# Attention in a macaron transformer: where VectorE frees a PSUM bank, and in which steps it adds gathered expert rows

## The reference, cut to what matters

```python
# mixture of experts: x = x + 0.5 * sum over the two best experts of weight * expert(norm(x))
# attention, on norm(x):
q = (x @ Wq + bq).reshape(b, t, H, hd).transpose(0, 2, 1, 3)
k = ((x @ Wk + bk) @ Wl + bl).reshape(b, t, H, lhd).transpose(0, 2, 1, 3)
v = ((x @ Wv + bv) @ Wl + bl).reshape(b, t, H, lhd).transpose(0, 2, 1, 3)
attn = jax.nn.softmax(jnp.einsum('bhqd,bhkd->bhqk', q, k) * scale, axis=-1)
out = jnp.einsum('bhqk,bhkd->bhqd', attn, v)
x = x + out.transpose(0, 2, 1, 3).reshape(b, t, L) @ Wo + bo
```

## Time and profile before

| | |
|---|---|
| median of 3 runs | 1384.77 us (1379.14 to 1384.81) |
| profiled execution, its own time | 1381.53 us |
| its span, first to last instruction | 1379.8 us |
| mean granted TensorE clock | 0.962 |
| busy over the span | PE 89%, DVE 81%, ACT 63%, POOL 37% |
| the chain that ended last, by engine | PE 54%, DVE 25%, issue 8%, ACT 8% |

### The profile page before, as it was taken

How to read it: one execution, slowest core, us unless ns; L and a number is a source line. 1 busy time by engine, 2 the same in 40 slices (tenths; PEclk the granted TensorE clock), 3 DMA queues, 4 the chain that set the end, 5 groups by cost and what they waited for, 6 DMA issues and landing times.

```text
span 1379.8 us, 22519 instructions
## 1 busy us (share of the span) xinstructions
PE 1227.8 (89%) x7168; PEld 776.2 (56%) x7168; DVE 1120.5 (81%) x2387; ACT 875.9 (63%) x1535; POOL 511.8 (37%) x762
## 2 busy tenths in 40 slices
PE   6767989678899879988889999899999899899998
PEld 5657989412322322222267999866666356656675
DVE  6865979789989979888767989978886787778885
ACT  6855777358788858887887777634343588234432
POOL 6772437544544506420373335605330220210100
PEclk9988999779999989999999999999999999999999
DMA  8595556522312203210263566456463010263535
GB/s 271 122 362 188 210 196 231 157 73 89 93 48 90 82 26 97 86 48 14 74 229 120 198 220 216 138 125 136 96 136 67 10 43 19 44 128 78 117 71 122
DMA packets 116608, 167.94 MB, mean 122 GB/s; under 512 B 18884, under 2 KB 63460, under 8 KB 115468
## 3 DMA queue, kind: packets, MB, share of 16 engines
q1 hardware_dynamic: 109324, 151.82, 37.7%
q0 software_dynamic: 7168, 14.69, 3.6%
HBM read 80.72 MB, written 45.09 MB: 91 GB/s over the span
## 4 chain that ended last, share of the span: by engine, by line
PE 54%; DVE 25%; issue 8%; ACT 8%; POOL 3%; DMA 2%; SPq 0%; DVEq 0%; ACTq 0%; POOLq 0%
PE bank L1703 8%; DVE shared L2326 6%; PE bank L2404 5%; PE pair L1615 4%; PE pair L1617 4%; PE pair L1616 3%; PE pair L955 3%; PE pair L957 3%; PE pair L2386 3%; PE pair L956 3%; PE pair L2318 3%; DVE shared L1039 3%; ACT shared L2394 2%; POOL xs_rows L649 2%; DVE shared L1037 2%
## 5 line engine op out<-in xcount | busy, mean ns | idle before, releaser
L2326 DVE TENSOR_REDUCE shared<-pair 128x2 f32<-128x1024 f32 x256 | 309.9, 1217 | 37.9 <-PE pair L2318 34.8
L2394 ACT ACTIVATE shared<-pair 128x1024 f32<-128x1024 f32 x256 | 260.6, 1021 | 49.8 <-PE pair L2386 48.0
L955 PE MATMUL pair<-shared 128*128 128x256 f32 (+1 forms) x704 | 225.5, 320 | 6.8 <-issue 3.6
L957 PE MATMUL pair<-shared 128*128 128x256 f32 (+1 forms) x704 | 215.9, 307 | 0.0
L956 PE MATMUL pair<-shared 128*128 128x256 f32 (+1 forms) x704 | 215.6, 306 | 0.0
L1039 DVE TENSOR_TENSOR shared<-shared 128x512 fp32r<-128x512 f32 x208 | 155.9, 757 | 56.3 <-ACT shared L1029 53.1
L1670 ACT ACTIVATE shared<-pair 128x512 f32<-128x512 f32 x144 | 84.6, 594 | 146.9 <-PE pair L1617 144.8
L1615 PE MATMUL pair<-shared 128*128 128x512 f32 x288 | 152.4, 529 | 0.2 <-DVE shared L1625 0.2
L1023 ACT ACTIVATE shared<-pair,shared 128x256 f32<-128x256 f32 x288 | 121.5, 477 | 48.9 <-PE pair L957 42.5
L955 PEld LDWEIGHTS pair<-shared 128*128 128x128 f32 x704 | 136.0, 193 | 15.0 <-issue 5.4
L2404 PE MATMUL bank<-shared 128*9 128x512 f32 x1024 | 137.1, 608 | 4.5 <-ACT shared L2394 4.3
(11 more groups left out here) (384 smaller groups left out, 2249.6 us busy)
## 6 DMA issues: line engine op xcount, KB each, us to landing
shared<-shared SPq DMA_DIRECT2D x144, 256.0 KB
shared<-p_coef_rows SPq DMA_DIRECT2D x64, 512.0 KB, 8.6
shared<-xs_rows SPq DMA_DIRECT2D x36, 256.0 KB, 3.0
ys_rows<-shared SPq DMA_DIRECT2D x36, 256.0 KB
w_keep<-shared SPq DMA_DIRECT2D x8, 1024.0 KB, 13.8
shared<-w_keep SPq DMA_DIRECT2D x16, 512.0 KB
shared<-p_q_parts SPq DMA_DIRECT2D x64, 96.0 KB, 2.3
shared<-p_k_parts SPq DMA_DIRECT2D x64, 96.0 KB, 2.4
```

Source lines behind the costliest of these rows:

```text
L955: nc.tensor.matmul(out_bank, w_hi, x_hi, start=start, stop=False)
L957: return nc.tensor.matmul(out_bank, w_lo, x_hi, start=False, stop=stop)
L2326: nc.vector.tensor_reduce(mneg[:, i, 2 * c:2 * c + 2], pair_of("max", b, m)[:], AX_X, ALU.max, negate=True).then_inc(s["mx_read"], 1)
L2394: nc.scalar.activation(probs[st % 2][:, 2 * p:2 * p + 2, :], pair_of("exp", b, 2 * st + p)[:], ACT.Exp, scale=scale).then_inc(s["exp_done" ...
```

## The change

VectorE's turn operations move in front of the maximum of the same slot, and the eight adds of a body move from slots 13 to 23 to slots 1 to 9. No operation is added or removed on any engine, and no size changes.

```diff
@@ -2561,17 +2561,22 @@
                         if st == 15:
                             norm_from(f0 + b + AHEAD, b + AHEAD, bank[7])
 
+            def turn_dve(v, b, at, first_):
+                st, j = divmod(at, 2)
+                if j == 0 and st % TILES == 3:
+                    if st > 3:
+                        o_dve(v, b, st // TILES - 1)
+                    elif not first_:
+                        o_dve(v, b - 1, GB - 1)
+                if at == 10 and not first_:
+                    z_dve(v, b - 1)
+                if at == 18 and b + FIRST < B:
+                    v_dve(v, b + FIRST, bank[7])
+
             def between_dve(v, b, st, j, first_):
                 g, kt = st // TILES, st % TILES
                 at = 2 * st + j
                 routed = routes is not None and not first_
-                if j == 0 and kt == 3:
-                    if st > 3:
-                        o_dve(v, b, g - 1)
-                    elif not first_:
-                        o_dve(v, b - 1, GB - 1)
-                if at == 10 and not first_:
-                    z_dve(v, b - 1)
                 if routed and b in PLACED_IN and at in PLACED_IN[b][1]:
                     G, pieces = PLACED_IN[b]
                     place, half = pieces[at]
@@ -2581,8 +2586,6 @@
                     seq_stats_a(v, routes, b - 1)
                 if routed and at == 12:
                     seq_stats_b(v, routes, b - 1)
-                if b + FIRST < B and at == 18:
-                    v_dve(v, b + FIRST, bank[7])
                 if b + AHEAD < B:
                     if at in COMBINE_AT:
                         combine_piece(v, occ0, b + AHEAD, COMBINE_AT.index(at))
@@ -2597,11 +2600,12 @@
                     if routes and b == B - 1 and st == 15:
                         weights_dense(v, routes)
 
-            COMBINE_AT = (13, 15, 16, 17, 19, 20, 21, 23)
+            COMBINE_AT = (1, 2, 3, 4, 5, 7, 8, 9)
 
             def dve_b(v, b, par, first_, last_):
                 for st in range(STEPS):
                     for j in range(2):
+                        turn_dve(v, b, 2 * st + j, first_)
                         if lagged(b, 2 * st + j):
                             max_dve(v, *lagged(b, 2 * st + j))
                         between_dve(v, b, st, j, first_)
```

## The result

The changed kernel takes 1373.45 us (median of 11 runs, 1369.73 to 1377.39), the kernel before 1381.27 in its own 11 (1378.97 to 1384.81): a ratio of 0.9946, 95% interval 0.993 to 0.9962. It is faster, by 7.5 us by that ratio (the medians are 7.8 apart), where 18.2 were forecast. Its profiled execution took 1375.78 us, span 1374.0.

The account below looks back on a forecast made before the run. TensorE and VectorE were both taken as within 10% of full, VectorE saturated in slots 11 to 25. Gains of 14.5 us in the bodies and 3.7 for the clock, 18.2 together, took 1384.77 to 1366.6 us; range 1359 to 1379.

Parts of the forecast that it names:

- What bounds the kernel: Attention bodies: TensorE and VectorE within 10% of full; VectorE has spare time in slots 0 to 9, none in 11 to 25.
- Part 1, which waits go: Turns before maxima: 23.2 of 25.6 us of TensorE's bank 7 waits can go; new VectorE waits priced at nothing.
- Part 1, what is given back: Bodies 1 and 2: late maxima delay score matmuls, 1.1 of 3.8 us lost, 2.7 gained each, about 47.0 us long.
- Body 6: Waits of 1.1 us go, less 0.5 at slot 30, where the score matmul waits for the delayed maximum: 0.6 gained.
- Body 3: Gains 2.7 us like bodies 1 and 2, and 1.2 at its end: 3.9.
- Part 2, the adds: Eight adds in bodies 0 to 4 move to early slots, costing nothing in bodies 0 to 3; body 4 gains 1.0 us from both parts.
- rival (d): Gathers block adds: three a body, up to 0.98 us each, 13 us over five bodies, half in idle time: 1373; chance 0.03.
- Part 3, the clock: End of body 3: gap shrinks from 2.57 to 1.35 us, so TensorE's clock no longer falls to half; 3.7 us gained.
- (a): The clock falls all the same at the end of body 3: 1370.3 us; chance 0.15.
- (b): Early slots have no room, VectorE becomes the bound there, adds cost 10.5 us of the gain: 1377; chance 0.10.
- (c): The order gives nothing, TensorE waits for later maxima instead of the bank; only collisions go: 1381; chance 0.13.
- (e): Adds and placement in slots 3 to 9 stretch TensorE gaps in bodies 0 to 4, the clock falls: 1393; chance 0.05.

Follow-up runs that it names:

- e2_adds: Only the adds moved, turn operations still behind the maximum, against the kernel before; 1378.31 us, ratio 0.9962.
- e3_pool: The changed kernel, with POOL splitting the maxima of group 3 before the gather of slot 15; 1369.37 us, ratio 0.9905 to the kernel before.
- e8_slot30: The changed kernel, with `o_dve` behind the maximum again in slot 30 of body 6 alone; 1372.82 us, ratio 0.9933 to the kernel before.
- e10_before: The kernel before, unchanged, measured and traced a second time; 1382.43 us, ratio 0.9991 to its earlier runs.
- e7_late4: The changed kernel, with the adds of body 4 alone back in slots 13 to 23; 1372.86 us, ratio 0.9934 to the kernel before.
- e1_turns: Only the turn order changed, adds still in slots 13 to 23, against the kernel before; 1375.70 us, ratio 0.9954.
- e9_after: The changed kernel, unchanged, measured and traced a second time; 1372.86 us, ratio 0.9930 to the kernel before.
- e11_place: Changed kernel with edits of e3_pool and e7_late4, pick_b in slot 31 of bodies 3 and 6, body 4's placement pieces spread out; 1364.29 us, ratio 0.9866.

## Why the prediction was right or wrong

**Direction and range** were right: 1373.45 us lies between 1359 and 1379. The size was not: 7.5 us (9.7 in the second measurement) against 18.2. There is luck in the absolute figure. The base of 1384.77 us, from three runs, was 3.5 us above the median of eleven; from 1381.27 the same sum gives 1363.1, and 1373.45 is 10.4 us above that.

**What bounds the kernel: right.** Spare VectorE time in slots 0 to 9, none in 11 to 25. VectorE's timeline before shows it. e2_adds agrees, with 1.2 us a body for the same eight adds, but does not prove it by itself, since 0.8 us of collisions with POOL goes with them.

**Part 1, which waits go: right.** Of 25.6 us in 38 waits about 4.5 are left in four waits: 1.44 and 1.35 us where I had said 1.35 and 1.0, one of 0.3, and one of 1.42 behind `z_dve` in body 4, which I had counted as gone. The price of the new waits of VectorE was right too: `z_dve` and `v_dve` never find their matmuls late in bodies 1 to 3.

**Part 1, what is given back: wrong, for POOL was left out.** I gave back 1.1 us in bodies 1 and 2 to score matmuls that meet a late maximum. There are none. What takes their place is POOL: 1.16 us in each of bodies 1 to 3 for the split of group 3's maxima, which I had dismissed with "ScalarE, SP and POOL get no operation and pass none". They pass none, but POOL's split was done only 0.2 us before `v_dve` let the transposes go, and that margin I did not look up, nor that POOL would not come earlier when TensorE did. Bodies 1 and 2 took 47.8; with POOL's order mended (e3_pool) 47.0. That this is the forecast length is luck in part: the 1.1 us are given back, but not to late maxima. Waits for exponentials take back 0.5 (1.0 us against 0.5 before), and the other 0.6 stays open. POOL is the whole miss in those bodies, 0.8 us each, and in body 3 as much again: 2.4 us.

**Body 5: 1.1 gained, 1.7 forecast. Body 6: 0.1 to 0.4 lost, 0.6 forecast as gain.** The 0.5 us at slot 30 was right (e8_slot30). In body 5 part of the waits that went came back as waits of `max_pe` for exponentials (0.5 us before, 1.0 after) and of a score matmul for a maximum (0.2), which I had priced too low; in body 6 the 1.1 us of waits that went brought nothing, and this was not followed further.

**Body 3: 2.2 gained at equal clock, 3.9 forecast.** Between e10_before (52.2 us) and e8_slot30 (50.0), neither with half clock at its end, POOL's wait takes 0.8 of the missing 1.7 and the new wait of 0.57 us for a maximum, right behind the gap of 1.44, another 0.6; 0.3 stays open.

**Part 2, the adds: right in bodies 1 to 3.** 0.34 us each, no collision there, and no sign that they cost anything in their new slots. The rule of the Trainium skill (SBUF — State Buffer, section "SBUF: two separate sides") decided nothing here: an add beside a gather takes 0.34 us, so rival (d) is out. Body 4 is the exception: I had taken 1.0 us of gain there from both parts. At equal clock it is 0.5 (55.1 in e10_before, 54.6 in e8_slot30), and e7_late4 against e8_slot30 puts the adds' share at some 0.3 us of loss.

**Part 3, the clock: the step that failed.** The forecast took the half clock after the gap of 2.57 us as belonging to the kernel, and gave 3.7 us for its going. It belongs to an execution. With the gap of 2.57 us it was there in two traces (the kernel before and e2_adds, 10.2 us each) and not in a third (e10_before). With 1.44 and 0.56 us it was there in two traces of the changed kernel (10.2 and 3.4 us) and not in e1_turns, e3_pool, e7_late4 and e8_slot30, which have the same two gaps. The price itself was right: bodies 3 and 4 together take 110.9 us in the kernel before and 107.4 in e10_before, 3.5 us apart, where I had 3.7. But the median mixes executions, so the going of the fall could not bring it whole. How often each kernel has the fall is not known from so few traces.

**The sum again, at equal clock.** The bodies were to gain 14.5 us. Taking e10_before against e8_slot30 for bodies 3 and 4, the mean of both traces of each kernel for body 6, the traces with 3.4 us of half clock for body 7, and the first traces otherwise, they gained, from body 0 to body 7, 1.4 + 3.8 (bodies 1 and 2) + 2.2 + 0.5 + 1.1 - 0.3 + 0 = 8.7. The missing 5.8 is POOL's 2.4, 0.9 more in body 3, 0.5 in body 4, 0.6 in body 5, 0.9 in body 6 and 0.5 in body 7. With nothing for the clock, 18.2 - 3.7 - 5.8 = 8.7 us lies inside both measured intervals (5.2 to 9.7 and 6.5 to 12.9 us). So the forecast fell short by two things: 5.8 us in the bodies and 3.7 for the clock.

**Rivals.** (a), the fall at the end of body 3 all the same, is what both traces of the changed kernel show, but it comes and goes. (b) and (c) are out in bodies 1 to 3: the adds cost nothing seen there, and the waits are gone. Of (d) the price was also mis-added: three gathers a body at 0.98 us are 14.7 us over five bodies, not 13. (e) is real in its mechanism (e2_adds, body 4), kept small by the turns in front.

By the medians the order and the adds give 7.1 and 4.5 us alone, and 7.8 and 10.5 together in the two measurements. In bodies 1 and 2 they nearly add up (0.5 + 1.2 against 1.9). What e1_turns gains beyond its bodies is not explained.

## What to carry to other kernels

When an operation that held a shared buffer moves forward, look up for every waiter not only what held it but what would have held it next, and by how much: 0.2 us of margin on an engine that is half busy took a third of the gain in those bodies. Where one engine is saturated for part of a loop and has gaps in another part, moving small work across can pay more than reordering it in place (here 1.2 against 0.5 us a body, with collisions in both figures), except where the target slots are full already. When small operations move, look also at what the other engine does beside them: part of the gain here is that POOL no longer stretches them. And before pricing a stretch of half clock as a gain, see it in a second trace.

## What the runs showed of the hardware

TensorE's clock fell or did not fall after the same sequence of matmuls and gaps. After 2.57 us of idle time: 10.2 us of half clock in two traces, none in a third. After 1.44 and 0.56 us: 10.2 and 3.4 us in two, none in four. After 2.66 us at the end of body 6: 10.2, 10.2, 6.8, 3.4 and 3.4 us (after, e1_turns, e7_late4, e3_pool, e9_after). A fall of 10.2 us cost 3.5 and 3.7 us in bodies 3 and 4 together (before against e10_before, after against e8_slot30). The scatter is not of the attention phase alone: behind it, where no edit reaches, the traces have 19 to 35 us of half clock and take 687.5 to 693.8 us. This is as large as the effect of a whole edit here, so a kernel with such gaps needs repeated traces. The version without half clock in its bodies 1 to 7 (e11_place) had four of five runs between 1364.08 and 1364.61 and the fifth at 1367.10; whether it is steadier, five runs can't say.

VectorE's add, which reads two tiles of SBUF, took 0.34 us alone and beside the gather's instruction of 0.95 us. Beside POOL's operations on SBUF it took 0.86 (L2056, 1.16 us), 1.22 (L2053, 1.17 us) and 0.94 us (L2451, 1.27 us).
